# A perceiver layer on one core: batch 0's scores moved ahead in the self attention, values as the stationary operand, residual sums before their norms, filling matmuls placed anew

## The chip, the cores and the metric

The kernel runs on one core of a Trainium2 chip. The metric is device time in microseconds. Three runs of the kernel before took 890.71, 892.66 and 893.37 us, median 892.66 us. Most executions of one kernel agree within 0.3 per cent (2.7 us here).

The engines of the core are TensorE (PE in the rows; its weight loads are PEld), VectorE (DVE), ScalarE (ACT), GpSimd (POOL) and SyncE (SP), which here issues nearly all DMAs. Each runs its own list of instructions in order, and they wait for each other by semaphores.

## The reference, cut to what matters

Everything is float32. B = 2 batches, L = 128 latent rows, D = 512 columns.

```
x = x + xattn(ctx_1024, layernorm(x), mask, ...)      # latents attend to 2048 context rows, 16 heads of 64
x = x + attn(layernorm(x), qw, kw, vw, ow)            # the self attention, where the change lies
x = x + ffn(layernorm(x), ...)                        # gated MLP of 2048, and product-key experts

def attn(x, qw, kw, vw, ow):                          # 16 heads of 32, batch 2, sequence 128
    Q, K, V = rope(x @ qw), rope(x @ kw), x @ vw
    score = Q @ K^T / sqrt(32) - 1e10 * (1 - causal)  # 128 x 128 for each head
    weights = softmax(score)
    return (weights @ V) @ ow
```

## The kernel before, in words

The program is written out by hand for each engine. Nothing is scheduled by a planner: the order of the calls in each engine's block is the order in which the engine works, and semaphores (`s_...`, `c_...` for compute, `d_...` for DMAs) tie the blocks together. Activations and weights of most products are kept as a high and a low part, and `product` (L1619 to L1623) issues three matmuls: high by high, high by low, low by high. An operand is split by a copy on ScalarE (`..._hi`) and a subtraction on VectorE (`..._lo`, L1096).

The span has three parts. The cross attention (from 0 to about 654 us) runs 48 iterations of a pair of heads. The self attention (about 652 to 716 us) is what the change rewrites. The feed-forward part (gated MLP, then 16 steps of experts) fills the rest. The weight blocks of the last two parts come by DMA (2 MB each where they are split already) into a few slots of SBUF, each issued once the block that used the slot last has been used (`wait_used`).

At the very start TensorE turns the first context chunk and the latents (`x_turn`, `latent`), and between these calls it runs ten matmuls whose results nobody reads: `occupy`, L1782 to L1785, filling matmuls that keep the engine busy. Then come the first query product `queries(0)` and the first keys `project_keys(0, 0)`.

The self attention works like this, b being the batch:

- `turn_rows` transposes a normalised 128x512 activation on TensorE in four pieces into a PSUM bank from `TBANK`. ScalarE's `transposed_hi` and VectorE's `transposed_lo` split it into `HT` (the input), `QTs` (queries), `KN` (keys) or `AT` (the attention's output).
- `project_rows(m, b)` is a product over four blocks of 128, twelve matmuls of 128x512: m = 0 queries, 1 keys, 2 values. `rotate(m, b)` applies the rotary embedding on VectorE; `values_hi(b)` copies the values to `VV` on ScalarE.
- `scores(b)` makes all 16 heads' scores in 48 matmuls of 32 rows. `row_max(g)` (VectorE, g = 4b + c, four heads each) adds the mask and takes the maximum, `exps(g)` (ScalarE) makes four exponentials with their sums, `turn_weights(g)` (TensorE) transposes them, `probs_copy(g)` copies them to `PV2`, and `weigh_values(g)` multiplies by the values.
- In the kernel before, `weigh_values` takes the 128x128 weights of a head as the stationary operand and streams 32 columns of values: the output has latent rows on partitions. VectorE's `norm_outputs(b)` divides by the sums (`AO`), and `turn_rows(AO, b)` transposes again before `mix_rows(b)`, the product with `ow`.
- `add_rows(i, b)` adds to the residual and takes the row statistics, GpSimd's `row_rstd(i, b)` makes the inverse deviation, `norm_rows(i, b)` normalises.

Around the stage's end VectorE's order is `norm_outputs(1)`, `add_rows(1, 0)`, `transposed_lo(AT, 1)`, `norm_rows(1, 0)`, the two low parts of the search keys `KBk`, `transposed_lo(HT, 0)`, `add_rows(1, 1)`, `norm_rows(1, 1)`, `transposed_lo(HT, 1)`. TensorE then makes the search queries (product with `fWq`, L1621 on `pS<-XA,WS`), with which the feed-forward part begins.

Of the kernel before, what the change touches and what calls it, by code (L numbers as in the profile page):

```python
# [26 lines left out]
ALU = mybir.AluOpType  # L27
ACT = mybir.ActivationFunctionType
AX = mybir.AxisListType

P = 128
# [4 lines left out]
def perceiver_layer(nc, x, ctx1024, mask, g1, b1, g2, b2, Wq, Wkv, Wout, qw, kw, vw, ow,  # L36
# [40 lines left out]
    with ExitStack() as stack:  # L77
# [155 lines left out]
        s_ao = sem("s_ao")  # L233
# [62 lines left out]
        AO = QR  # L296
# [33 lines left out]
        TBANK = (pJ[:, 0, :], pJ[:, 0, :], pT[:, 1, :], pX, pX, pV, pX, pV, pX, pV)  # L330
# [64 lines left out]
        def _(sp):  # L395
# [180 lines left out]
            sp.wait_ge(s_tt, 10)  # L576
# [26 lines left out]
        def _(pool):  # L603
# [133 lines left out]
            gp.memset(KV[:, 0:1024].bitcast(U32), 0).then_inc(s_kz, 1)  # L737
            pool.wait_ge(s_sc, 8)
# [8 lines left out]
            last.then_inc(s_iota, 1)  # L747
            for b in range(B):
                row_rstd(1, b)
# [17 lines left out]
        def _(act):  # L767
# [198 lines left out]
            def transposed_hi(dst, b):  # L966

                act.wait_ge(s_tt, nb[0] + 1)
                ac.activation(dst[:, HI, :, L * b:L * b + L], TBANK[nb[0]].rearrange("p (c t) -> p c t", c=4), ACT.Copy).then_inc(s_th, 1)
                nb[0] += 1  # L970

            def values_hi(b):
# [4 lines left out]
                ac.activation(VV[:, b, :], (pT[:, 0, :], pJ[:, 0, :])[b], ACT.Copy).then_inc(s_vh, 1)  # L977
# [8 lines left out]

            joined_hi(ITERS - 2)
            transposed_hi(HT, 0)
            joined_hi(ITERS - 1)
            transposed_hi(HT, 1)  # L990
            transposed_hi(QTs, 0)
            values_hi(0)
            transposed_hi(KN, 0)
            exps(0)
            exps(1)
            values_hi(1)
            transposed_hi(QTs, 1)
            transposed_hi(KN, 1)
            for g in range(2, 8):
                exps(g)  # L1000
            transposed_hi(AT, 0)
            transposed_hi(AT, 1)
# [82 lines left out]
        def _(dve):  # L1085
# [274 lines left out]
            def rotate(m, b):  # L1360
# [5 lines left out]
                z = ((pS[:, 0, :], pS[:, 1, :]), (pV, pJ[:, 1, :]))[b][m].rearrange("p (h e two) -> p h e two", h=SH, two=2)  # L1366
# [26 lines left out]
            def probs_copy(g):  # L1393
# [4 lines left out]
                ve.tensor_copy(PV2[:, g % 4, :], pJ[:, (g + 1) % 2, :]).then_inc(s_p2h, 1)  # L1398
# [38 lines left out]
            probs_copy(5)
            transposed_lo(AT, 0)
            probs_copy(6)
            probs_copy(7)  # L1440
            norm_outputs(1)
            add_rows(1, 0)
            transposed_lo(AT, 1)
            norm_rows(1, 0)
            dve.wait_ge(s_kh, 1)
# [3 lines left out]
            transposed_lo(HT, 0)  # L1449
            add_rows(1, 1)  # L1450
            norm_rows(1, 1)
            transposed_lo(HT, 1)
# [163 lines left out]
        def _(pe):  # L1616
# [165 lines left out]
            def occupy(bank, weights, moving, n):  # L1782

                for _ in range(n):
# [378 lines left out]
```

## Time and profile before

| what | value |
|---|---|
| median of three runs | 892.66 us |
| the profiled execution | 892.87 us, span 891.1 us, so 1.8 us lie outside the span |
| TensorE busy | 851.9 us (96%) |
| VectorE, ScalarE, GpSimd busy | 579.7 us (65%), 437.5 us (49%), 349.0 us (39%) |
| granted TensorE clock, mean | 0.995 of full speed |
| the chain of waits, by engine | PE 81%, DVE 10%, issue 3%, ACT 3%, DMA 2%, POOL 1% |

The span counts from the first instruction to the last. A matmul's end is modelled and matmuls are pipelined, so a full TensorE is not one at its peak. Filling matmuls count as busy. Line numbers are those of the kernel before.

### The profile page before, as it was taken

Reading aid. Unit: us, or ns where it says so; the run is one execution under the profiler, and the core shown is the slowest. Engines: PE = TensorE matmul, PEld = TensorE weight load, DVE = VectorE, ACT = ScalarE, POOL = GpSimd, SP = SyncE. Lnnn points to the kernel's source line nnn. Section 1 sums busy time; section 2 is a strip of 40 time slices with the busy share of each in tenths; the row PEclk is TensorE's granted clock in tenths of the full one; section 3 lists DMA queues with packets and bytes.
Section 4 is the critical chain, followed back from the end, with each engine's and each line's share of the span. In section 5 each row is a group of like instructions: output and inputs, shape, how many; then the busy total and the mean of one; then the engine's idle time right before and its main releaser. Section 6 shows DMA issues by size and latency. Waiting matters only on the chain.

```text
span 891.1 us, 17432 instructions
## 1 busy us (share of the span) xinstructions
PE 851.9 (96%) x6353; PEld 794.7 (89%) x6353; DVE 579.7 (65%) x1540; ACT 437.5 (49%) x1017; POOL 349.0 (39%) x362
## 2 busy tenths in 40 slices
PE   3899999999999999999999999999989999998997
PEld 2889999999999999999999999999967789987885
DVE  7445555566576878756566666777767546746885
ACT  4465554545546455544646454455425224334552
POOL 5634523645353664745454453413211110003442
PEclk9999999999999999999999999999999999999999
DMA  6365336457566677575666755887578366842310
GB/s 200 95 221 172 120 130 224 177 192 231 197 237 239 242 234 272 200 236 195 234 215 213 238 192 191 292 336 246 207 295 329 136 257 262 352 143 89 101 48 25
DMA packets 71109, 183.04 MB, mean 205 GB/s; under 512 B 6336, under 2 KB 19568, under 8 KB 65008
## 3 DMA queue, kind: packets, MB, share of 16 engines
q1 hardware_dynamic: 70928, 181.90, 57.8%
q8 instruction: 51, 0.84, 0.4%
q14 instruction: 34, 0.28, 0.1%
q10 hardware_dynamic: 96, 0.02, 0.0%
HBM read 130.00 MB, written 50.86 MB: 203 GB/s over the span
## 4 chain that ended last, share of the span: by engine, by line
PE 81%; DVE 10%; issue 3%; ACT 3%; DMA 2%; POOL 1%; SPq 0%; DVEq 0%; ACTq 0%; POOLq 0%
PE pJ L1621 15%; PE pJ L1622 14%; PE pJ L1623 14%; PE pV L1751 8%; PE pS L1729 4%; PE pT L1737 3%; PE pS L1737 3%; PE pT L1729 2%; PE pS L1621 2%; PE pS L1622 2%; PE pS L1623 2%; PE pX L1652 1%; DVE late L1578 1%; DMA WS<-w_split 1%; PE pV L1621 1%
## 5 line engine op out<-in xcount | busy, mean ns | idle before, releaser
L1621 PE MATMUL pJ<-WV,XT 128*128 128x256 f32 x544 | 159.2, 293 | 0.0
L1622 PE MATMUL pJ<-WV,XT 128*128 128x256 f32 x544 | 154.5, 284 | 0.0
L1623 PE MATMUL pJ<-WV,XT 128*128 128x256 f32 x544 | 154.4, 284 | 0.0
L848 ACT ACTIVATE SP<-SP,xneg 128x768 f32<-128x768 f32 (+1 forms) x96 | 85.8, 895 | 119.5 <-DVE xneg L1200 119.5
L1621 PE MATMUL pJ<-XT,WK 128*128 128x384 f32 (+1 forms) x384 | 126.9, 330 | 3.9 <-DVE VT L1096 2.9
L1623 PE MATMUL pJ<-XT,WK 128*128 128x384 f32 (+1 forms) x384 | 125.2, 326 | 0.0
L1622 PE MATMUL pJ<-XT,WK 128*128 128x384 f32 (+1 forms) x384 | 125.1, 326 | 0.0
L1096 DVE TENSOR_TENSOR KT<-pJ,KT 128x384 fp32r<-128x384 f32 x96 | 51.1, 535 | 90.8 <-ACT KT L825 90.3
L1621 PEld LDWEIGHTS pJ<-WV,XT 128*128 128x128 f32 x544 | 104.8, 193 | 0.5 <-issue 0.2
L1622 PEld LDWEIGHTS pJ<-WV,XT 128*128 128x128 f32 x544 | 104.9, 193 | 0.0
L1623 PEld LDWEIGHTS pJ<-WV,XT 128*128 128x128 f32 x544 | 104.8, 193 | 0.0
L649 POOL TENSOR_TENSOR XT<-xtmp,XT 128x384 fp32r<-128x384 f32 (+1 forms) x44 | 41.4, 940 | 135.8 <-ACT XT L809 135.6
L832 ACT ACTIVATE VT<-pJ 128x512 fp32r<-128x512 f32 (+1 forms) x72 | 41.2, 573 | 86.8 <-PE pJ L1623 86.8
L825 ACT ACTIVATE KT<-pJ 128x384 fp32r<-128x384 f32 x96 | 44.9, 469 | 69.1 <-PE pJ L1623 69.1
L1751 PE MATMUL pV<-PT,VT 128*128 128x256 f32 x544 | 77.5, 291 | 0.0
L1621 PEld LDWEIGHTS pJ<-XT,WK 128*128 128x128 f32 x384 | 72.3, 188 | 5.6 <-DVE VT L1096 4.4
L1751 PEld LDWEIGHTS pV<-PT,VT 128*128 128x128 f32 x544 | 67.6, 189 | 10.2 <-issue 8.0
L1096 DVE TENSOR_TENSOR VT<-pJ,VT 128x512 fp32r<-128x512 f32 (+1 forms) x72 | 47.2, 656 | 40.0 <-ACT VT L832 39.6
L1622 PEld LDWEIGHTS pJ<-XT,WK 128*128 128x128 f32 x384 | 72.4, 189 | 0.0
L1623 PEld LDWEIGHTS pJ<-XT,WK 128*128 128x128 f32 x384 | 72.2, 188 | 0.0
L1194 DVE CUSTOM_DVE_ANT_0 SP<-pS,MB,mx 128x384 f32<-128x384 f32 x64 | 36.9, 615 | 50.8 <-PE pS L1729 50.8
L759 POOL TENSOR_TENSOR late<-late 128x512 f32<-128x512 f32 x16 | 20.6, 1288 | 111.9 <-DVE late L1578 111.9
(374 smaller groups left out, 2171.5 us busy)
## 6 DMA issues: line engine op xcount, KB each, us to landing
WS<-w_split SPq DMA_DIRECT2D x14, 2048.0 KB, 8.9
WV<-wv_split SPq DMA_DIRECT2D x20, 1024.0 KB, 7.0
WK<-wk_split SPq DMA_DIRECT2D x40, 512.0 KB, 4.4
w_split<-wkst SPq DMA_DIRECT2D x40, 512.0 KB, 3.3
w_split<-wvst SPq DMA_DIRECT2D x40, 512.0 KB, 3.8
XA<-w_split SPq DMA_DIRECT2D x4, 2048.0 KB, 12.9
xraw<-in_ctx SPq DMA_DIRECT2D x7, 768.0 KB, 6.4
wk_split<-WK SPq DMA_DIRECT2D x8, 512.0 KB, 3.8
```

The lines of the kernel that those rows point to most:

```text
L649: gp.tensor_tensor(XT[:, C % 4, LO, k, c0:c0 + w], xtmp[:, e % 2, 0:w], XT[:, C % 4, HI, k, c0:c0 + w].bitcast(F32), ALU.subtract).then_in ...
L825: ac.activation(KT[:, q, HI, 0:w], pJ[:, j % 2, 0:w], ACT.Copy).then_inc(c_jh, 1)
L832: ac.activation(VT[:, G % 2, ts[0]:ts[-1] + 1, :, HI, :], pJ[:, j % 2, 0:256 * len(ts)].rearrange("p (t h e) -> p t h e", t=len(ts), h=4), ...
L848: ac.activation(SP[:, I % 2, h, 0:w], SP[:, I % 2, h, 0:w], ACT.Exp, bias=xneg[:, I % 2, h:h + 1], scale=XSC, accum_out=total).then_inc(c_ ...
L1096: return ve.tensor_tensor(dst, src, hi.bitcast(F32), ALU.subtract)
L1194: ve.tensor_tensor_reduce(out=SP[:, n % 2, h, c0:c0 + w], in0=BANK[2 * q + h][:, 0:w], in1=MB[:, c0:c0 + w], scale=1.0, scalar=before, op0 ...
L1621: te.matmul(dst, a(HI), b(HI), start=start, stop=False)
L1622: te.matmul(dst, a(HI), b(LO), start=False, stop=False)
L1623: return te.matmul(dst, a(LO), b(HI), start=False, stop=stop)
L1729: last = te.matmul(BANK[2 * q + h][:, 0:w], Q[rows, qs, p, :], KT[rows, q, ks, 0:w], start=o == 0, stop=o == 2)
L1737: last = te.transpose(BANK[t % 4][:, P * i:P * i + P], SP[:, I % 2, h, CWID * q + P * i:CWID * q + P * i + P], ident[:, :])
L1751: last = te.matmul(pO[:, h, :, :], VT[:, G % 2, 3 * q + i, 2 * (I % 2) + h, :, :], PTS[t % 4][:, :, P * i:P * i + P], start=q == 0 and i = ...
```

## The change

It has five parts, all by hand.

1. The ten filling matmuls ahead of `queries(0)` are gone.
2. In the self attention the queries and keys of batch 0 are rotated, turned and split before the input of batch 1 is, and `scores(0)` comes before any product of batch 1. The value product of batch 0 and that of batch 1 are cut into halves with turns between them. The four `probs_copy` of batch 0 move from VectorE to ScalarE. `transposed_lo(KN, 1)` now stands ahead of `row_max(4)` to `row_max(7)`, which follow each other without copies between.
3. `weigh_values` takes 32 columns of values as the stationary operand and streams the 128 columns of turned weights; head h of the four writes partitions 32h to 32h + 31. The output comes out transposed, so `turn_rows(AO, b)` is dropped. For the division the inverse sums must be on the other axis: VectorE's `invert`, GpSimd's `repeat_inverses` (a copy that repeats each inverse 32 times), TensorE's `turn_inverses` (four transposes), ScalarE's `inverse_rows` (a copy to SBUF), then VectorE multiplies in place in PSUM and ScalarE's `weighed_hi` and the low part follow.
4. `add_rows(1, 1)` stands ahead of `norm_rows(1, 0)`, and the low parts of `KBk` behind both splits of `HT`.
5. The filling matmuls of the self attention are 4 + 3 + 3 + 3 inside and 9 + 2 + 5 before the search queries (before: 4 + 4 + 4 + 4 + 4, and 16 + 5); the five behind the search queries stay.

```diff
-        AO = QR
+        IROW = QR
+        RBANK = (pV[:, :], pS[:, 0, :])
...
-        TBANK = (pJ[:, 0, :], pJ[:, 0, :], pT[:, 1, :], pX, pX, pV, pX, pV, pX, pV)
+        TBANK = (pJ[:, 0, :], pT[:, 1, :], pX, pJ[:, 0, :], pJ[:, 1, :], pV, pX, pV, pX, pV)
+        PBANK = (pJ[:, 0, :],) * 4 + (pJ[:, 1, :], pJ[:, 0, :]) * 2
...
+            def repeat_inverses(b):
+
+                pool.wait_ge(s_inv, b + 1)
+                gp.tensor_copy(an[:, b, :].rearrange("p (h e) -> p h e", h=SH),
+                               small[:, 32 + 16 * b:48 + 16 * b].unsqueeze(2).broadcast_to([P, SH, SD])).then_inc(s_rep, 1)
...
+            def probs_copy(g):
+
+                act.wait_ge(s_pt2, g + 1)
+                ac.activation(PV2[:, g % 4, :], PBANK[g], ACT.Copy).then_inc(s_p2h, 1)
+
+            def inverse_rows(b):
+
+                act.wait_ge(s_row, b + 2)
+                ac.activation(IROW[:, b, :], RBANK[b], ACT.Copy).then_inc(s_rowc, 1)
...
             def norm_outputs(b):
 
-                dve.wait_ge(s_se, 4 * b + 4)
-                inv = small[:, 32 + 16 * b:48 + 16 * b]
-                link(ve.reciprocal(inv, small[:, 16 * b:16 * b + 16]))
+                dve.wait_ge(s_rowc, b + 2)
                 dve.wait_ge(s_pv2, 4 * b + 4)
-                ve.tensor_tensor(AO[:, b, :].rearrange("p (h e) -> p h e", h=SH), OUT2[b].rearrange("p (h e) -> p h e", h=SH),
-                                 inv.unsqueeze(2).broadcast_to([P, SH, SD]), ALU.mult).then_inc(s_ao, 1)
+                ve.tensor_tensor(OUT2[b][:, :], OUT2[b][:, :], IROW[:, b, :], ALU.mult).then_inc(s_ao, 1)
...
             def weigh_values(g):
 
                 b, c = g // 4, g % 4
+                pe.wait_ge(s_vh, b + 1)
                 pe.wait_ge(s_p2h, g + 1)
                 for h in range(4):
                     cs = slice(SD * (4 * c + h), SD * (4 * c + h) + SD)
-                    last = te.matmul(OUT2[b][:, cs], PV2[:, g % 4, P * h:P * h + P], VV[:, b, cs], start=True, stop=True)
+                    last = te.matmul(OUT2[b][ROWS4[h], P * c:P * c + P], VV[:, b, cs], PV2[:, g % 4, P * h:P * h + P], start=True, stop=True)
                 last.then_inc(s_pv2, 1)
...
+            def turn_inverses(b):
+
+                pe.wait_ge(s_rep, 4 + b + 1)
+                if b == 1:
+                    pe.wait_ge(s_sm, 8)
+                for c in range(4):
+                    last = te.transpose(RBANK[b][:, P * c:P * c + P], an[:, b, P * c:P * c + P], ident[:, :])
+                last.then_inc(s_row, 1)
```

TensorE around the first scores, before: the last products of a whole projection of batch 1's keys (`pJ<-WS,XA`), then the scores (`pS` and `pT<-KNs,XA`, 24 such rows), then the values of batch 1.

```order
L1621 MATMUL pJ<-WS,XA 128x512
L1622 MATMUL pJ<-WS,XA 128x512
L1623 MATMUL pJ<-WS,XA 128x512
L1903 MATMUL pS<-KNs,XA 128x128 x2
L1903 MATMUL pT<-KNs,XA 128x128 x2
```

The same place in the changed kernel (L1906 are transposes of `late`, the rotated keys, and `raw`, the input of batch 1):

```order
L1906 MATMUL pX<-ident,late 128x128 x4
L1906 MATMUL pJ<-ident,raw 128x128 x4
L1656 MATMUL pV<-WS,XA 128x512
L1657 MATMUL pV<-WS,XA 128x512
L1658 MATMUL pV<-WS,XA 128x512
L1656 MATMUL pV<-WS,XA 128x512
L1657 MATMUL pV<-WS,XA 128x512
L1658 MATMUL pV<-WS,XA 128x512
L1935 MATMUL pS<-KNs,XA 128x128 x2
L1935 MATMUL pT<-KNs,XA 128x128 x2
```

Only the second half of batch 0's values is left ahead of the scores, and batch 1's queries and keys have moved behind them.

TensorE from the second batch's first weighed values to the product with `ow` (`pX<-WS,XA`), before:

```order
L1927 MATMUL pX<-xst,PVs 128x32 x8
L1785 MATMUL pJ<-WS 128x512 x4
L1918 MATMUL pJ<-ident,SMs 128x128 x4
L1876 MATMUL pX<-ident,late 128x128 x4
L1918 MATMUL pJ<-ident,SMs 128x128 x4
L1927 MATMUL pV<-xst,PVs 128x32 x8
L1785 MATMUL pJ<-WS 128x512 x4
L1918 MATMUL pJ<-ident,SMs 128x128 x8
L1927 MATMUL pV<-xst,PVs 128x32 x8
L1621 MATMUL pX<-WS,XA 128x512
```

and in the changed kernel (L1948 turns weights, L1958 weighs values, L1967 turns inverses, L1900 fills):

```order
L1948 MATMUL pJ<-ident,SMs 128x128 x4
L1958 MATMUL pV<-PVs,xst 32x128 x4
L1900 MATMUL pJ<-WS 128x512 x3
L1948 MATMUL pJ<-ident,SMs 128x128 x4
L1958 MATMUL pV<-PVs,xst 32x128 x4
L1900 MATMUL pJ<-WS 128x512 x3
L1948 MATMUL pJ<-ident,SMs 128x128 x4
L1967 MATMUL pS<-ident,O 128x128 x4
L1958 MATMUL pV<-PVs,xst 32x128 x8
L1656 MATMUL pX<-WS,XA 128x512
```

The turns go singly and the last turn is followed by the inverses; the turn of the output (L1876) is gone.

VectorE at the end of the stage, before (`XA<-pV` and `XA<-pX` are low parts, `O<-xres` the norms):

```order
L1406 TENSOR_TENSOR late<-pV,small 128x512
L1257 TENSOR_TENSOR xres<-pX,xres 128x512
L1258 BN_STATS st<-xres 128x6
L1259 BN_AGGR mv<-st 128x2
L1096 TENSOR_TENSOR XA<-pV,XA 128x4x128
L1264 TENSOR_SCALAR O<-xres,mv,rstd 128x512
L1096 TENSOR_TENSOR KV<-pT,KV 64x4x64 x2
L1096 TENSOR_TENSOR XA<-pX,XA 128x4x128
L1257 TENSOR_TENSOR xres<-pV,xres 128x512
L1258 BN_STATS st<-xres 128x6
L1259 BN_AGGR mv<-st 128x2
L1264 TENSOR_SCALAR O<-xres,mv,rstd 128x512
```

and in the changed kernel:

```order
L1444 TENSOR_TENSOR pV<-pV,late 128x512
L1131 TENSOR_TENSOR XA<-pV,XA 128x4x128
L1292 TENSOR_TENSOR xres<-pX,xres 128x512
L1293 BN_STATS st<-xres 128x6
L1294 BN_AGGR mv<-st 128x2
L1292 TENSOR_TENSOR xres<-pV,xres 128x512
L1293 BN_STATS st<-xres 128x6
L1294 BN_AGGR mv<-st 128x2
L1299 TENSOR_SCALAR O<-xres,mv,rstd 128x512 x2
L1131 TENSOR_TENSOR XA<-pX,XA 128x4x128
L1131 TENSOR_TENSOR XA<-pV,XA 128x4x128
L1131 TENSOR_TENSOR KV<-pT,KV 64x4x64 x2
```

The low part of the second output is now first, and the second residual sum has nothing but the first in front of it.

## Rows read from the trace of the kernel before

**Rows 1.** The page, part 4: the chain by engine

```profile
PE 81%; DVE 10%; issue 3%; ACT 3%; DMA 2%; POOL 1%; SPq 0%; DVEq 0%; ACTq 0%; POOLq 0%
```

**Rows 2.** Windows: length, busy PE, PEld, DVE, ACT, POOL, clock, DMA, GB/s

```profile
20.10:22.00 1.90, 1.69 (x12) 1.49 (x12) 1.83 (x5) 1.40 (x4) 1.82 (x3) 1.00 1.03 387
28.00:33.00 5.00, 5.00 (x33) 5.00 (x32) 2.50 (x7) 2.60 (x5) 2.02 (x2) 0.66 0.19 56
660.00:716.20 56.20, 49.65 (x359) 40.55 (x357) 36.44 (x131) 19.19 (x77) 8.33 (x20) 1.00 0.67 269
```

**Rows 3.** Timeline, TensorE at the start: start, length, instruction, idle before and releaser

```profile
12.06 2.06 PE L1785 MATMUL pS<-WQs 128*128 128x512 f32 x4
...
20.15 0.38 PE L1621 MATMUL pJ<-XL,WQs 128*128 128x256 f32 x1 [1.35 <-POOL XL L673]
...
22.92 0.41 PE L1621 MATMUL pJ<-XT,WK 128*128 128x384 f32 x1 [1.08 <-issue]
...
27.49 0.55 PE L1652 MATMUL pX<-ident,Oacc 128*128 128x128 f32 x3 [2.24 <-ACT Oacc L913]
```

**Rows 4.** Timeline, VectorE in the self attention

```profile
662.01 0.39 DVE L1370 TENSOR_TENSOR late<-pS,rope 128x256 f32<-128x256 f32 x1
...
664.22 0.55 DVE L1264 TENSOR_SCALAR raw<-xres,mv,rstd 128x512 f32<-128x512 f32 x1
...
686.25 0.29 DVE L1386 CUSTOM_DVE_ANT_0 SMs<-pS,cmask 128x128 f32<-128x128 f32 x1 [1.30 <-PE pT L1903]
...
687.30 0.28 DVE L1386 CUSTOM_DVE_ANT_0 SMs<-pS,cmask 128x128 f32<-128x128 f32 x1
...
710.89 0.68 DVE L1257 TENSOR_TENSOR xres<-pV,xres 128x512 f32<-128x512 f32 x1
...
713.58 0.55 DVE L1264 TENSOR_SCALAR O<-xres,mv,rstd 128x512 f32<-128x512 f32 x1 [1.06 <-POOL rstd L730]
```

**Rows 5.** Timeline, TensorE in the self attention, and one row of the experts

```profile
663.75 0.50 PE L1621 MATMUL pT<-WS,XA 128*128 128x512 f32 x1 [0.69 <-DMA WS<-w_split]
...
674.84 0.32 PE L1903 MATMUL pS<-KNs,XA 32*128 32x128 f32 x2
...
684.56 0.33 PE L1903 MATMUL pS<-KNs,XA 32*128 32x128 f32 x2
...
686.05 1.97 PE L1927 MATMUL pX<-xst,PVs 128*128 128x32 f32 x16
687.86 1.19 PE L1785 MATMUL pJ<-WS 128*128 128x512 f32 x4
...
700.82 0.48 PE L1621 MATMUL pX<-WS,XA 128*128 128x512 f32 x1
...
706.12 0.50 PE L1621 MATMUL pV<-WS,XA 128*128 128x512 f32 x1 [1.47 <-DVE XA L1096]
...
709.02 0.60 PE L1876 MATMUL pX<-ident,O 128*128 128x128 f32 x4
709.37 3.90 PE L1785 MATMUL pS<-WS 128*128 128x512 f32 x16
...
716.25 0.39 PE L1621 MATMUL pS<-XA,WS 128*128 128x256 f32 x1 [0.27 <-DVE XA L1096]
...
806.61 0.69 PE L2116 MATMUL pS<-exrow,delta 1*128 1x256 f32 x2
```

**Rows 6.** Timeline, ScalarE: the last pair of exponentials and what follows it

```profile
691.93 0.40 ACT L983 ACTIVATE SMs<-SMs,negm 128x128 f32<-128x128 f32 x1 [1.31 <-DVE negm L1391]
...
695.03 0.58 ACT L969 ACTIVATE XA<-pX 128x512 fp32r<-128x512 f32 x1
```

**Rows 7.** Groups by form, GpSimd: count, busy us, mean ns, idle before

```profile
L661 POOL TENSOR_SCALAR xraw<-xraw,mv,rstd 128x512 f32<-128x512 f32 x27 | 56.2, 2095 | 0.9
...
L625 POOL CAST wvst<-wvst 128x512 fp32r<-128x512 f32 x40 | 25.3, 633 | 2.3 <-DMA wvst<-in_L_ffn_Wu 1.6 <-DMA wvst<-in_L_ffn_Wg 0.4 <-DMA wvst<-in_L_attn_qw 0.2
```

**Rows 8.** The page, part 6: weight blocks, KB each, us to landing

```profile
WS<-w_split SPq DMA_DIRECT2D x14, 2048.0 KB, 8.9
```

More of the change, by code:

```diff
@@ L989, in _ @@
             joined_hi(ITERS - 1)
+            transposed_hi(QTs, 0)
+            transposed_hi(KN, 0)
             transposed_hi(HT, 1)
-            transposed_hi(QTs, 0)
             values_hi(0)
-            transposed_hi(KN, 0)
             exps(0)
             exps(1)
+            probs_copy(0)
+            exps(2)
+            probs_copy(1)
+            transposed_hi(QTs, 1)
+            exps(3)
+            transposed_hi(KN, 1)
+            probs_copy(2)
             values_hi(1)
-            transposed_hi(QTs, 1)
-            transposed_hi(KN, 1)
-            for g in range(2, 8):
+            probs_copy(3)
+            exps(4)
+            inverse_rows(0)
+            for g in range(5, 8):
                 exps(g)
-            transposed_hi(AT, 0)
-            transposed_hi(AT, 1)
+            weighed_hi(0)
+            inverse_rows(1)
+            weighed_hi(1)
             act.wait_ge(s_kt, 1)
@@ L1780, in latent @@
                 last.then_inc(c_lt, 1)
-            def occupy(bank, weights, moving, n):
-                for _ in range(n):
-                    te.matmul(bank, weights, moving, start=True, stop=True)
-            first_q = WQs[:, 0, HI, :, :].rearrange("p k n -> p (k n)")
             x_turn(0, 0)
             x_turn(0, 1)
-            pe.wait_ge(c_wqh, 1)
-            occupy(pS[:, 0, :], WQs[:, 0, HI, 0, :], first_q, 4)
             latent(0)
             latent(1)
-            occupy(pS[:, 0, :], WQs[:, 0, HI, 0, :], first_q, 2)
             latent(2)
@@ L1870, in _, with occupy @@
                     queries(I + 2)
+            def occupy(bank, weights, moving, n):
+                for _ in range(n):
+                    te.matmul(bank, weights, moving, start=True, stop=True)
             def turn_rows(src, b, ready, count):
@@ L1877, in turn_rows @@
                 last.then_inc(s_tt, 1)
-                nb[0] += 1
+                nb[0] += 3 if nb[0] == 5 else 1
             def last_rows(k0, k1, joined):
@@ L1950, in _ @@
+            project_rows(0, 1)
+            turn_weights(0)
+            pe.wait_ge(s_vh, 1)
             project_rows(1, 1)
-            scores(0)
-            project_rows(2, 1)
             turn_rows(QR, 1, s_rope, 3)
+            turn_weights(1)
+            weigh_values(0)
+            pe.wait_ge(s_sm, 4)
+            project_rows(2, 1, (0, 1))
             turn_rows(KR, 1, s_rope, 4)
-            turn_weights(0)
-            weight_ready(5)
-            pe.wait_ge(s_vh, 2)
-            occupy(pJ[:, 0, :], slot4(5, HI)[:, 0, 0:P], slot4(5, HI)[:, 0, :], 4)
@@ L1959, in _ @@
-            turn_weights(1)
-            pe.wait_ge(s_tl, 5)
-            occupy(pX[:, :], slot4(5, HI)[:, 0, 0:P], slot4(5, HI)[:, 0, :], 4)
-            scores(1)
-            weigh_values(0)
+            turn_weights(2)
             weigh_values(1)
-            occupy(pJ[:, 1, :], slot4(5, HI)[:, 0, 0:P], slot4(5, HI)[:, 0, :], 4)
-            turn_weights(2)
+            project_rows(2, 1, (2, 3))
             turn_weights(3)
             weigh_values(2)
+            scores(1)
+            turn_inverses(0)
```

132 lines of the change are left out of this document (74 added, 58 removed).

## The prediction, made before the changed kernel ran

> **What bounds the kernel now.** I read the chain of waits by engine first: TensorE holds 81% of it [rows 1]. So what counts is where TensorE waits, and the windows show it: in the stretch from 660.0 to 716.2 us, the self attention, it is busy 49.65 of 56.2 us, the granted clock is 1.00, and DMA is at 0.67 [rows 2]. That busy time flatters the stretch, since it counts filling matmuls, 16 of which take 3.90 us, 0.24 us each, in front of the search queries [rows 5]. The timeline shows three waits. The first scores start at 674.84 us; the second at 684.56; VectorE can begin the second softmax only at 686.25, after 1.30 us idle [rows 4, 5]. ScalarE's exponentials of batch 1 are interrupted (1.31 us idle before the last pair) and end at 695.03 [rows 6]. The product with `ow` of batch 0 starts at 700.82, that of batch 1 only at 706.12 after waiting 1.47 us for a low part, and the search queries at 716.25 [rows 5]. All four are ends of one serial story, so I walk it again in the new order. Outside it nothing of the order of work changes except at the start.
>
> **Unit prices.** A product of twelve matmuls behind a wait: 709.02 - 706.12 = 2.90 us, and 2.85 without one; half of it 1.45. Four transposes: 709.37 - 709.02 = 0.35, I take 0.40 with the change of operands. 48 score matmuls: 686.05 - 684.56 = 1.49. Two `weigh_values` in the old form: 687.86 - 686.05 = 1.81, 0.90 each [rows 5]. A `row_max`: 687.30 - 686.25 = 1.05. A rotation: 664.22 - 662.01 = 2.2. A residual sum with statistics: 713.58 - 710.89, less the 1.06 of waiting for GpSimd, 1.6. A norm: 0.55 [rows 4]. An `exps`: (695.03 - 691.93) / 2 = 1.55; a ScalarE copy: 0.58, 0.48 when others follow [rows 6]. I add 0.1 to 0.2 us for each semaphore between engines.
>
> **Batch 0's scores first.** TensorE ends the keys of batch 0 at 663.1 (663.75 less 0.69 of waiting) as before. Rotation (0,0) now stands ahead of the residual sum, so queries are ready at 660.9 and turned at 663.5; the value weights land at 663.7, where TensorE waited for them before [rows 5], and half the value product runs to 665.2. VectorE: residual sum to 662.5, rotation (1,0) 663.1 to 665.3, norm of batch 1's input to 665.9. Keys turned at 665.8, split at 667.4; in between TensorE turns batch 1's input and does the other value half, to 667.75. Scores start at 667.75, 7.1 us sooner than 674.84.
>
> **Up to the second scores.** From 669.25 TensorE has three projections of batch 1 (3 x 2.85), five turns (2.0), three `weigh_values` and two or three short waits. With 0.6 us for a weighing that is 8.55 + 2.0 + 1.8 + 0.8 = 13.2, so the second scores start at 682.5 instead of 684.56: 2.0 us. ScalarE (four `exps`, three copies of 0.48, three splits and the values: 9.9 us from 670.6) and VectorE are done just before. The moved 7.1 us are mostly spent here: the same TensorE work, but now under batch 0's softmax instead of ahead of it.
>
> **Batch 1's softmax.** VectorE has the four `row_max` in a row, 684.2 to 688.4, and ScalarE then never waits: `exps(4)` from 685.4, four times 1.55 plus one copy of the turned inverses 0.48, end 692.1 against 695.03. That is 2.0 from before, 1.3 for the idle that is gone, 0.48 given back: 2.9 us in all. Cover: turns, weighings and fills lie under the exponentials.
>
> **Up to the product with `ow`.** Before, from 695.03 to 700.82, 5.8 us: two turns of weights after a late weighing and fills, two copies, two weighings of 0.9. Now only `turn_weights(7)` and the inverses are left: turn 693.1, inverse sums ready at 692.5, GpSimd's copy, turned inverses, two weighings of 0.6: product at 695.1. So 3.0 us from 692.1 to 695.1, a gain of another 2.8; 5.7 in all. GpSimd's copy is not in the trace: its plain copy of 128x512 takes 0.63 and its two-scalar operation on the same size 2.10 [rows 7]. I take 0.65, as it has one input; then TensorE's turns of `exps(7)` cover nearly all of it. The upper end costs 1.4 us.
>
> **From one `ow` product to the other.** 5.3 us before: product 2.85, turn, ScalarE's split, and the low part behind a residual sum on VectorE. The second output now needs no turn and its low part stands first, so it is split (697.3) before the first product ends (697.95); then the keys' turn 0.4 and the product at 698.4 instead of 706.12. 2.0 us more, 7.7 in all.
>
> **To the search queries.** Product ends 701.25. From the residual sum at 710.89 to the queries at 716.25 took 5.36 us, and this chain (sum, GpSimd, norm, turn, split, low part) stays as it is, with batch 0's norm lying in GpSimd's share. But before, the sum began 1.9 us behind the product's end (709.02), because a low part stood ahead of it; now 0.15. Queries at 701.3 + 5.4 = 706.7 us, against 716.25: 9.5 us. The low parts of `KBk` (0.85 us) lie under the queries.
>
> **The weighing.** The new form is in no row. Its bounds: 48 score matmuls of 128 columns on a quarter of the array come every 31 ns (1.49 / 48), which with eight passes and an entry of about 0.25 gives 0.5 us; the one fp32 product with a wide moving operand takes 0.69 us for its two passes of 256 columns [rows 5], without the entry 0.11 us for 128 columns and a pass, so eight passes one after the other and the entry give 1.1; the old 0.90 lies between. I take 0.6, near the score row because here too each quarter of the array has its own operand. Five weighings lie on the path: -0.5 to +2.5 us. On TensorE's side the trace shows only row groups running together. The Trainium skill (TensorEngine Tiling (Array Packing), Tiling Modes, Key Properties) says that tiles work in parallel but that "Changing tiling mode (not just tile) drains the TensorE"; the first half speaks for the low bound, the second against the change, since every weighing now goes into such a mode and out. No row here prices a switch with 32 columns of output.
>
> **The start.** The first four fillers took 2.06 us, 0.51 each against 0.24 later, so TensorE was at its lower level of 1.2 GHz then; the first query product ran at the full clock; the values of 28 to 33 us, after idling 2.24 us, have a granted clock of 0.66 [rows 2, 3, 5]. Without fillers queries (twelve of 256 columns) and keys (twelve of 384) would run at half rate: they begin at 20.2 and 23.0, the keys end by 27.0 and the turns wait for ScalarE until 27.49 anyway [rows 3]. So the loss is hidden, by at least 0.4 us. And TensorE, then busy to 27 rather than 25, may keep or get the full clock for the values: 5 us at 0.66 hold 1.7 us to win; if it stays low longer, 1.0 to lose. I take 0.5 gained. The Trainium skill (TensorE: Matmul & The Clock Gate, Part 4) holds that transposes don't count as work for the clock; by that the queries do start at half rate, and the sum is the same by it.
>
> **Hidden ends.** The feed-forward's weights: a block lands 8.9 us after its issue [rows 8]; the first gate block's issue goes by batch 1's keys (1 us later than before), more than 25 us ahead of its use, and later ones go by uses that move along.
>
> **Sum.** 892.87 (the profiled execution; the median, 892.66, is 0.2 under it) - 9.5 - 0.5 = 882.9 us.
>
> **Rivals.** (a) *Weighing and inverses dear.* Weighings of 1.1 and a GpSimd copy of 2.1 us: 882.9 + 2.5 + 1.4, about 886.8. For it: no row for either. Against: one-input copies of this size are all 0.63. 13%. (b) *The gain is not passed on*: the stage ends sooner but the first gate products or experts wait for weights or selections, leaving under 2.7 us: about 891. Against: in the rows of the self attention's end only compute releases TensorE. 4%. (c) *Slower, by the clock.* Six gaps of 0.5 to 1 us on TensorE between 685 and 695 with fewer fillers (29 against 41) lower the granted clock to 1.2 GHz from there to the search queries. The path then holds about 2 x 2.9 of `ow`, 3 of weighings and turns and 5.8 of search queries at double time: 14 us lost, 897. It decides from the point where the low clock covers 9.5 us or more of TensorE work on the path. Against: the stretch kept 1.00 with a busy share of 0.88 [rows 2], and the gaps I find are no longer than its own. 4%. (d) *More gained*: weighings at 0.5 and all values at full clock, 881.2; 12%. (e) The walk holds: 67%.
>
> **Chances and range.** This kernel's runs tell 0.3% (2.7 us) from no change. Faster: e, a, d and nothing else, 0.92; same: b, 0.04; slower: c, 0.04. Range: d's low edge 880.5 to a's end 887.0.
>
> **What would show it.** Right: first scores near 667.8, second near 682.5, ScalarE's last exponential ending near 692, `ow` products at 695 and 698.4, search queries at 706.7 of the span. A weighing's four matmuls (eight passes) read in one row of the timeline; GpSimd's `small` copy likewise. Wrong if TensorE's idle before `turn_inverses(1)` exceeds 0.3 us, if the windows from 685 to 707 show a clock under 1.00, or if the distance from the search queries to the end, 174.8 us before, grows.

## The result, and the profile after

The changed kernel takes 881.38 us (median of 4 runs, 880.55 to 882.77), the kernel before, run beside it, 893.01. The ratio is 0.9866 with an interval of 0.9826 to 0.9906: 11.6 us by the medians or 1.3% faster, where 10.0 and a time of 882.9 had been forecast. On another chip, in a later comparison (`after_again` below), the ratio was 0.9882 (0.9865 to 0.9900), 10.5 us. One of the twelve executions of `start_fill_off` below took 4682.81 us and isn't counted in its ratio.

The profiled execution took 880.55 us, the shortest of the four; its span is 878.8 us. First the page's chain by engine, which answers to [rows 1]:

```profile
PE 79%; DVE 8%; DMA 4%; issue 3%; ACT 3%; POOL 1%; SPq 1%; DVEq 0%; ACTq 0%; POOLq 0%
```

TensorE still sets the end. The windows that answer to [rows 2] (length, busy PE, PEld, DVE, ACT, POOL, clock, DMA share, GB/s):

```profile
20.10:22.00 1.90, 1.82 (x8) 1.82 (x9) 1.86 (x5) 1.45 (x3) 1.82 (x4) 1.00 0.77 278
28.00:33.00 5.00, 5.00 (x42) 4.58 (x41) 2.81 (x10) 4.16 (x8) 3.24 (x4) 1.00 0.02 5
660.00:703.40 43.40, 40.46 (x334) 29.64 (x332) 29.67 (x117) 22.58 (x83) 9.39 (x21) 1.00 0.77 306
```

The second line is new: the values at the start run at a clock of 1.00 where it was 0.66. The clock of the first can't be taken at its word: the products in it come every 0.21 to 0.22 us, as the rows below show (20.56, 20.78), where the same product of 256 columns comes every 0.12 us at the full clock (31.22, 31.34 us), so they run at the lower level. The third line is busy for 0.93 of its time, against 0.88.

TensorE in the self attention, by the timeline (start, length, instruction, idle before and releaser); the rows answer to [rows 5]:

```profile
652.25 0.50 PE L1656 MATMUL pS<-WS,XA 128*128 128x512 f32 x1 [0.86 <-DVE XA L1131]
...
664.99 0.33 PE L1935 MATMUL pS<-KNs,XA 32*128 32x128 f32 x2
...
673.24 0.60 PE L1948 MATMUL pJ<-ident,SMs 128*128 128x128 f32 x4
673.77 0.42 PE L1958 MATMUL pX<-PVs,xst 128*32 128x128 f32 x8
674.13 0.50 PE L1656 MATMUL pT<-WS,XA 128*128 128x512 f32 x1
...
679.35 0.33 PE L1935 MATMUL pS<-KNs,XA 32*128 32x128 f32 x2
...
683.92 0.66 PE L1948 MATMUL pJ<-ident,SMs 128*128 128x128 f32 x4 [0.94 <-ACT SMs L993]
...
686.03 0.63 PE L1948 MATMUL pJ<-ident,SMs 128*128 128x128 f32 x4 [0.76 <-DVE PVs L1433]
...
690.56 0.77 PE L1958 MATMUL pV<-PVs,xst 128*32 128x128 f32 x16
691.41 0.50 PE L1656 MATMUL pX<-WS,XA 128*128 128x512 f32 x1
...
694.79 0.50 PE L1656 MATMUL pV<-WS,XA 128*128 128x512 f32 x1
...
703.42 0.38 PE L1656 MATMUL pS<-XA,WS 128*128 128x256 f32 x1 [0.26 <-DVE XA L1131]
```

VectorE and ScalarE there, by the same view, answering to [rows 4] and [rows 6]:

```profile
681.04 0.29 DVE L1421 CUSTOM_DVE_ANT_0 SMs<-pS,cmask 128x128 f32<-128x128 f32 x1 [3.19 <-PE pT L1935]
...
697.85 0.69 DVE L1292 TENSOR_TENSOR xres<-pV,xres 128x512 f32<-128x512 f32 x1 [1.70 <-PE pV L1658]
```

```profile
688.87 0.58 ACT L1010 ACTIVATE XA<-pX 128x512 fp32r<-128x512 f32 x1
```

VectorE waits for the second scores longer than before (3.19 us against 1.30 [rows 4]), and batch 1's residual sum follows its product with nothing between. TensorE's first row is a product ahead of all that moved in this stage. The same product started at 655.12 us before:

```profile
655.12 0.49 PE L1621 MATMUL pS<-WS,XA 128*128 128x512 f32 x1 [0.86 <-DVE XA L1096]
```

So 2.87 us had been gained by then, at the start; to compare the stage with my walk, they are added back:

| step | before | predicted | after | after + 2.87 |
|---|---|---|---|---|
| first scores | 674.84 | 667.75 | 664.99 | 667.86 |
| second scores | 684.56 | 682.5 | 679.35 | 682.22 |
| ScalarE's last exponential ends | 695.03 | 692.1 | 688.87 | 691.74 |
| product with `ow`, batch 0 | 700.82 | 695.1 | 691.41 | 694.28 |
| product with `ow`, batch 1 | 706.12 | 698.4 | 694.79 | 697.66 |
| search queries | 716.25 | 706.7 | 703.42 | 706.29 |

The stage gave 9.96 us where 9.5 stood in the sum, the start 2.87 where 0.5 stood, and the rest took 175.4 us instead of 174.8, within its scatter (174.1 to 176.2 over fourteen profiles). Together 12.3 us of span. Two prices that no row had shown are read above and here: a weighing is 0.36 us (673.77 to 674.13; 690.56 to 691.41 holds two and a wait), and GpSimd's copy is 0.61, both times that it runs:

```profile
677.92 0.61 POOL L743 COPY O<-small 128x512 f32<-128x512 f32 x1 [16.61 <-DVE small L1438]
```

The start is where my working missed. TensorE after:

```profile
14.72 0.69 PE L1814 MATMUL pX<-ident,SP 128*128 128x128 f32 x2 [2.32 <-DVE SP L1175]
...
20.18 0.58 PE L1656 MATMUL pJ<-XL,WQs 128*128 128x256 f32 x1 [1.63 <-POOL XL L675]
20.56 0.42 PE L1657 MATMUL pJ<-XL,WQs 128*128 128x256 f32 x1
20.78 0.42 PE L1658 MATMUL pJ<-XL,WQs 128*128 128x256 f32 x1
...
25.95 0.55 PE L1687 MATMUL pX<-ident,Oacc 128*128 128x128 f32 x3
```

The queries run at half rate, as forecast. But the turns of `Oacc` come at 25.95 us, straight behind the keys, and not at 27.49 [rows 3]. What they wait for is ScalarE's norm, and that waits for VectorE's `nmr`. ScalarE in the kernel before:

```profile
25.21 2.22 ACT L913 ACTIVATE Oacc<-Oacc,nmr,rstd 128x512 f32<-128x512 f32 x3 [2.89 <-DVE nmr L1296]
```

VectorE in the kernel before:

```profile
17.15 1.03 DVE L1123 CAST XT<-OF 128x256 fp32r<-128x256 f32 x2
...
20.99 1.84 DVE L1096 TENSOR_TENSOR XT<-Oacc,XT 128x256 fp32r<-128x256 f32 x2
22.75 2.30 DVE L1096 TENSOR_TENSOR WV<-wvst,WV 128x1024 fp32r<-128x1024 f32 x1
24.97 0.15 DVE L1296 SCALAR_TENSOR_TENSOR nmr<-mv,rstd 128x3 f32<-128x3 f32 x1
```

and after:

```profile
17.13 0.50 DVE L1158 CAST XT<-OF 128x256 fp32r<-128x256 f32 x2
...
20.52 0.76 DVE L1131 TENSOR_TENSOR XT<-Oacc,XT 128x256 fp32r<-128x256 f32 x2
21.20 1.22 DVE L1131 TENSOR_TENSOR WV<-wvst,WV 128x1024 fp32r<-128x1024 f32 x1
22.33 1.24 DVE L1331 SCALAR_TENSOR_TENSOR nmr<-mv,rstd 128x3 f32<-128x3 f32 x1
```

The same low part takes 2.30 or 1.22 us, the small `nmr` 0.15 or 1.24. GpSimd in the kernel before and after shows what lies beside them:

```profile
21.24 1.30 POOL L637 TENSOR_TENSOR WQs<-wqst,WQs 128x512 fp32r<-128x512 f32 x1
22.50 1.47 POOL L633 TENSOR_TENSOR WK<-wkst,WK 128x512 fp32r<-128x512 f32 x1
```

```profile
21.66 1.89 POOL L639 TENSOR_TENSOR WQs<-wqst,WQs 128x512 fp32r<-128x512 f32 x1
```

As the rows read, the two engines hold each other up, and the row that starts second is the long one. Before, GpSimd's `WK` row starts first (22.50) and VectorE's low part is long. After, VectorE's part starts first (21.20), GpSimd's row is long (1.89), and `nmr`, begun at 22.33, is done only when that row ends, 23.55 us. `before_nmr_first` below shows the same pair the other way round. That it is access to memory which one engine withholds from the other is not shown by any run here. The Trainium skill (Advanced Engine Details and Errata, VectorE Performance Modes) says of VectorE's two-port instructions that they and GpSimd's "will interfere/block eachother", since the second port is shared; its table there gives `tensor_tensor` no two-port mode, so for the subtraction here, 2.30 against 1.22 us, it is near the case and doesn't state it.

What shifted their meeting is small: ScalarE's first split of the latents starts at 15.45 us instead of 15.23, because the transposes ahead of it run at the low clock now, and GpSimd's rows behind it shift by the same 0.22. The two VectorE sequences part at the cast of `XT` in the rows above: before it lies beside a GpSimd row that starts at 17.24 and takes 1.03 us for its two, after it is over in 0.50 before GpSimd's starts at 17.46. By the turns of `Oacc` it is worth 1.5 us.

### The profile page after: what moved, and what is told of

It is laid out like the page before. It is cut to its first block, busy times and chain, and to the rows that moved or that the text cites. A ratio compares the mean times of both kernels' runs of the same rounds, so it can differ in the third digit from the quotient of the medians.

```text
span 878.8 us, 17399 instructions
## 1 busy us (share of the span) xinstructions
PE 844.0 (96%) x6331; PEld 785.3 (89%) x6331; DVE 575.0 (65%) x1536; ACT 440.7 (50%) x1023; POOL 350.7 (40%) x364
## 4 chain that ended last, share of the span: by engine, by line
PE 79%; DVE 8%; DMA 4%; issue 3%; ACT 3%; POOL 1%; SPq 1%; DVEq 0%; ACTq 0%; POOLq 0%
PE pJ L1656 14%; PE pJ L1657 14%; PE pJ L1658 14%; PE pV L1786 7%; PE pS L1764 4%; PE pT L1772 3%; PE pS L1772 3%; PE pT L1764 2%; PE pS L1656 2%; PE pS L1658 2%; PE pS L1657 2%; DMA w_split<-wvst 1%; PE pX L1687 1%; DVE late L1613 1%; PE pV L1656 1%
```

## The experiments

Twelve runs in three comparisons, each with its own runs of the kernel before on the same chip; ratios are to these. "Stage" is the distance from the first scores to the search queries in the profile: 38.43 us in the changed kernel.

### The start: start_fill_back, start_fill_off, before_nmr_first, fill_nmr_first

```diff
             x_turn(0, 1)
+            pe.wait_ge(c_wqh, 1)
+            occupy(pS[:, 0, :], WQs[:, 0, HI, 0, :], first_q, 4)
             latent(0)
             latent(1)
+            occupy(pS[:, 0, :], WQs[:, 0, HI, 0, :], first_q, 2)
...
             x_turn(0, 3)
+            occupy(pS[:, 0, :], WQs[:, 0, HI, 0, :], first_q, 4)
             queries(0)
```

> The changed kernel with the ten filling matmuls put back ahead of the first query product; all else as changed. Theory A (the fillers cost the whole 2.9 us seen in the first 33 us): about 881.4 + 2.9 = 884.3 us, first scores of the cross attention at 33.3 us of the span, a granted clock near 0.66 in the values and VectorE's nmr near 25.0. Theory B (the part of it that comes from VectorE, 1.5 us, is a matter of how its operations fall beside GpSimd's in one execution and not of the fillers): about 882.9, the scores at 31.8.

Ratio 0.9882 (0.9862 to 0.9903), 883.7 us, but from 880.21 to 885.63 over five runs. The profiled one is the 880.21, and it speaks against theory A's mechanism: with the fillers in place the turns start at 25.99 us and `nmr` is early. The median lies near theory A's 884.3, but the five spread too far to tell it from 882.9. Its clock came late: a pair of latent transposes takes 0.69 us, as without fillers (0.44 before).

```profile
14.76 0.69 PE L1814 MATMUL pX<-ident,SP 128*128 128x128 f32 x2 [0.62 <-DVE SP L1175]
...
25.99 0.55 PE L1687 MATMUL pX<-ident,Oacc 128*128 128x128 f32 x3 [1.99 <-ACT Oacc L923]
```

So the fillers don't cost the 2.9 us each time. As I read it, they make it a matter of the execution whether the clock has risen by 14.7 us; where it has, the transposes are fast and VectorE meets GpSimd badly. The second half rests on one profile: of the four with these fillers only that of the kernel before has the fast transposes.

The reverse, the ten fillers taken out of the kernel before:

> The kernel before without its ten filling matmuls ahead of the first query product, nothing else changed. Theory A: 893.0 - 2.9 = 890.1 us, ScalarE's Oacc norm from 23.7 instead of 25.2 us and all values at the full clock. My forecast's term said 0.5 us (892.5). Rival: the self attention's new order carries all of the gain and the start nothing, 893.0.

0.9970 (0.9954 to 0.9986): 2.7 us faster, 1.3 to 4.1. Theory A's 2.9 lies in the interval, my forecast's 0.5 does not. The profile has the turns at 26.01 us and the cross attention's first scores at 30.34, as the changed kernel has (30.28), against 33.31 before.

```diff
-            dve.wait_ge(c_wvh, 1)
-            low(WV[:, 0, LO], wvst[:, :, :], WV[:, 0, HI]).then_inc(c_wv0, 1)
             dve.wait_ge(c_rstd, 2)
             ve.scalar_tensor_tensor(nmr[:, 0:3], ...).then_inc(s_nmr, 1)
+            dve.wait_ge(c_wvh, 1)
+            low(WV[:, 0, LO], wvst[:, :, :], WV[:, 0, HI]).then_inc(c_wv0, 1)
```

> The kernel before, fillers kept, with VectorE's nmr (what ScalarE's norm of Oacc waits for) ahead of WV's low part instead of behind it. If it is VectorE's late nmr that held the turns to 27.49 us, the turns start when the keys end (25.3), TensorE no longer idles 2.24 us, and with the full clock in the values (1.7 us) up to 3.9 us come back: 889.1 us. If only the clock counted and it stays at 0.66, 2.2 us: 890.8. If the turns wait for something else: 893.0.

0.9978 (0.9965 to 0.9991): 2.0 us faster, 0.8 to 3.1. In the profile the turns start at 25.25 us and the cross attention's first scores at 29.58, so its start is 3.7 us better than the one profiled before. But the clock came late in this execution too (0.69 us for a pair of latent transposes), so the profile doesn't show the collision avoided: the turns are 0.7 us sooner than `start_fill_back`'s. The case for `nmr` is the median of twelve: with the fillers kept, its place alone brought 2.0 us. The median got less than 3.7, probably because not every execution of the kernel before meets the collision. And here VectorE's low part starts just ahead of GpSimd's `WK` row, keeps its length, and GpSimd's is the long one, against 2.30 and 1.47 in the kernel before:

```profile
22.80 1.21 DVE L1096 TENSOR_TENSOR WV<-wvst,WV 128x1024 fp32r<-128x1024 f32 x1
```

```profile
22.81 2.33 POOL L633 TENSOR_TENSOR WK<-wkst,WK 128x512 fp32r<-128x512 f32 x1
```

> The changed kernel with the ten fillers back and nmr ahead of WV's low part: queries and keys at the full clock (keys end 25.3 instead of 25.9) and the turns not held. Expected 0.6 us faster than the changed kernel, 880.8, if both theories of the start hold; 884.3 if nmr's place is without effect; 882 to 883 if the low clock in the values comes back all the same.

0.9853 (0.9834 to 0.9871), 880.92 us, 880.16 to 882.62: the lowest median of all runs, and 880.8 was expected. Its interval overlaps with both of the changed kernel's, so that it is better isn't shown.

### The weighing: after_again, old_weigh_form

> The changed kernel itself, as the measure for the three others on the same chip. Expected: 0.987 of the kernel before, and in most executions full clock and early nmr at the start, since without fillers the transposes ahead of the queries are slow each time.

0.9882 (0.9865 to 0.9900), 882.65 us. The start was as expected (turns at 26.12), but the profile brought what my rival (c) had described: the clock fell inside batch 1's softmax, behind the same two gaps of 0.94 and 0.76 us that the other execution had passed at 1.00.

```profile
682.00:686.90 4.90, 3.54 (x31) 2.12 (x23) 4.51 (x37) 3.47 (x16) 4.16 (x12) 1.00 0.99 415
687.00:690.30 3.30, 3.06 (x16) 1.98 (x17) 1.47 (x3) 3.30 (x19) 0.81 (x2) 0.54 1.01 425
```

The second line has 0.54, about the lower level of 1.2 GHz; from 690.4 to 706.0 us it is 0.99 again. Stage: 39.92 instead of 38.43, so 1.49 us of this kernel's time come and go with it. A clock under 1.00 between 685 and 707 us was one of my signs of being wrong; this execution shows it, the other doesn't.

```diff
-   te.matmul(OUT2[b][ROWS4[h], P * c:P * c + P], VV[:, b, cs], PV2[:, g % 4, P * h:P * h + P], ...)
+   te.matmul(OUT2[b][:, cs], PV2[:, g % 4, P * h:P * h + P], VV[:, b, cs], ...)
```

> The changed kernel with weights as stationary operand again in the eight weighings (the old form: 32 columns moving through 128 by 128), so the weighed values come out untransposed and what is copied from them is another number; everything else is as changed. Theory A: the form's price, 0.90 us in place of 0.36, lies on the path for the three weighings ahead of the second scores and the last two, 5 x 0.54 = 2.7 us slower than the changed kernel. Theory B: the weighings wait for the copies of the turned weights anyway, so at most the last two count: 1.1 us or less.

0.9898 (0.9883 to 0.9913), 884.16 us, 1.5 us over `after_again` by the medians. The profiles say it more sharply, since the start and the clock drop out: the stage is 40.78 us against 38.43. The second scores are 1.12 us later, the first product with `ow` 2.39. This is theory A, a little under its 2.7: one weighing is 0.91 us in the old form, but enters 0.09 us sooner behind a turn (0.44 instead of 0.53).

```profile
681.52 0.60 PE L1948 MATMUL pJ<-ident,SMs 128*128 128x128 f32 x4
681.96 0.98 PE L1958 MATMUL pX<-xst,PVs 128*128 128x32 f32 x8
682.87 0.33 PE L1935 MATMUL pS<-KNs,XA 32*128 32x128 f32 x2
```

### The tail: tail_old, tail_both

```diff
-            transposed_lo(AT, 1)
             add_rows(1, 0)
-            add_rows(1, 1)
+            transposed_lo(AT, 1)
             norm_rows(1, 0)
-            norm_rows(1, 1)
-            transposed_lo(HT, 0)
-            transposed_lo(HT, 1)
...
+            transposed_lo(HT, 0)
+            add_rows(1, 1)
+            norm_rows(1, 1)
+            transposed_lo(HT, 1)
```

(the dots are `KBk`'s low parts)

> The changed kernel with VectorE's last steps in the old order: batch 0's residual sum ahead of the second output's low part, KBk's low parts and batch 0's norm and low part ahead of batch 1's sum. Theory A (my sum: 2.0 us at the second product with ow and 1.7 at the residual sum): the second product starts 1.9 to 2.0 us later, the search queries 3.5 to 3.7 us later. Theory B: the waits of the tail are hidden by TensorE's fillers and GpSimd's share, under 1 us.

0.9957 (0.9943 to 0.9971), 6.3 us over `after_again`. The second product is 1.99 us later, as in theory A, but the stage is 44.90 us, 6.5 longer. Neither theory fits: TensorE was left in the new order, where nine fillers stand ahead of batch 0's turn, and VectorE's low part of that turn now stands ahead of batch 1's residual sum. So the sum waited for fillers, and behind the idle time the clock fell to 0.50 between 706.8 and 710.1 us.

```profile
703.20 0.69 DVE L1131 TENSOR_TENSOR XA<-pX,XA 128x512 fp32r<-128x512 f32 x1 [4.07 <-ACT XA L979]
703.80 0.68 DVE L1292 TENSOR_TENSOR xres<-pV,xres 128x512 f32<-128x512 f32 x1
```

Hence the same with TensorE's order undone too:

```diff
-            occupy(pT[:, 1, :], searcher[:, 0:P], searcher, 9)
             turn_rows(hn, 0, s_src, 3)
-            occupy(pT[:, 1, :], searcher[:, 0:P], searcher, 2)
+            occupy(pT[:, 1, :], searcher[:, 0:P], searcher, 11)
```

> VectorE's last steps in the old order as in tail_old, and TensorE's too (batch 0's turn straight behind the second product with ow, all fillers behind it). Theory A: the extra 3 us of tail_old came from this mismatch, and the old tail on both engines costs what I had summed: second product 1.9 to 2.0 us later, search queries 41.9 us behind the first scores instead of 38.4, so 3.5 us slower than the changed kernel. Theory B: the old tail costs 6 us also with TensorE's order, and my sum was short by half.

0.9918 (0.9889 to 0.9946), 887.3 us: 5.4 us over `nmr_more_fill` on the same chip, 3 to 5 us over the changed kernel by the ratios. The second product is 1.94 us later. The stage is 43.43 instead of the expected 41.9, and the windows have the difference: the new wait of 1.91 us was followed by a fall of the clock in the middle of the product.

```profile
698.98 0.50 PE L1656 MATMUL pV<-WS,XA 128*128 128x512 f32 x1 [1.91 <-DVE XA L1131]
```

```profile
686.00:699.80 13.80, 10.88 (x81) 7.51 (x82) 8.46 (x27) 7.65 (x32) 4.06 (x9) 1.00 0.70 292
699.90:703.20 3.30, 3.30 (x10) 2.51 (x9) 1.17 (x3) 0.00 (x0) 0.00 (x0) 0.50 0.03 7
```

3.3 us at 0.50 and busy throughout hold 1.65 us; 43.43 - 1.65 = 41.8. Theory A's price of the old tail holds, with the clock's share on top. Its other half, that 3 us of `tail_old` were the mismatch, doesn't come out of the profiles: the two stages are 1.5 us apart (44.90 and 43.43, each with one fall of the clock), the ratios 3.5 us with intervals that just touch.

### The early scores: late_scores, late_scores_both

```diff
-            scores(0)
             pe.wait_ge(s_tl, 4)
             project_rows(0, 1)
-            turn_weights(0)
             pe.wait_ge(s_vh, 1)
             project_rows(1, 1)
+            scores(0)
+            turn_weights(0)
             turn_rows(QR, 1, s_rope, 3)
```

> The changed kernel with batch 0's scores behind the query and key products of batch 1 instead of ahead of them (5.7 us later, same instructions). Theory A (the early scores let the softmax of batch 0 run under batch 1's products): second scores 2.0 to 2.5 us later because three exponentials, copies and weighings of batch 0 then end last, and all later times with them. Theory B (TensorE has the same work either way, the order is worth nothing): no change within 0.3 us.

0.9961 (0.9944 to 0.9978), 7.6 us over `after_again`: both theories are wrong. The scores start at 672.64 us (`after_again` 666.20), and from them to the second scores it still takes 15.76 us (14.36), because TensorE waits twice:

```profile
677.21 0.80 PE L1948 MATMUL pJ<-ident,SMs 128*128 128x128 f32 x4 [3.01 <-ACT SMs L993]
679.72 1.11 PE L1906 MATMUL pJ<-ident,late 128*128 128x128 f32 x4 [1.71 <-DVE late L1410]
```

The first wait is for batch 0's exponentials, with nothing left to lay under them; the second for a rotation that stands behind three `row_max` on VectorE. And from 677.2 to 684 us the clock is at 0.53.

```diff
+            rotate(0, 1)
             row_max(0)
             row_max(1)
             row_max(2)
-            rotate(0, 1)
             row_max(3)
             rotate(1, 1)
```

(on top of `late_scores`)

> Batch 0's scores behind two products of batch 1 as in late_scores, and VectorE's rotation of batch 1's queries ahead of the four row_max instead of behind three, so that TensorE's turn of them no longer waits 1.7 us. Theory A: late_scores lost 1.4 us of its 8 to that wait and to the clock, so this one is 5 to 6 us slower than the changed kernel (first scores 6.9 us later, 12.5 to 13.5 instead of 14.4 us from there to the second). Theory B (the order of the scores is worth only what I had counted up to the second scores): 2.0 us slower.

0.9928 (0.9901 to 0.9955), 887.98 us: 6.1 us over `nmr_more_fill`, 4 to 6 over the changed kernel by the ratios. The wait for the rotation is gone, that for the exponentials stays at 3.12 us, and from the first to the second scores it takes 13.43 us, as theory A has it. Behind the wait the clock falls once more:

```profile
676.70:680.00 3.30, 3.21 (x16) 2.48 (x20) 3.20 (x18) 3.30 (x16) 0.00 (x0) 0.50 1.03 439
```

Counted from the turn of batch 0's queries, which both kernels start alike (661.21 and 662.54 us), the second scores are 4.8 us later than in `nmr_more_fill` (24.29 against 19.50). The wait is 3.12 of that and the clock 1.6: the products of batch 1 lie under batch 0's softmax or they don't.

### The fillers: nmr_more_fill, no_fill_att

The first has the start's edit of `before_nmr_first` and

```diff
-            occupy(PBANK[4], mixer[:, 0:P], mixer, 4)
+            occupy(PBANK[4], mixer[:, 0:P], mixer, 7)
...
-            occupy(PBANK[5], mixer[:, 0:P], mixer, 3)
+            occupy(PBANK[5], mixer[:, 0:P], mixer, 5)
```

> The changed kernel with two repairs: VectorE's nmr ahead of WV's low part at the start, and five more filling matmuls in batch 1's softmax (7 in place of 4 ahead of turn_weights(4), 5 in place of 3 ahead of turn_weights(5)), which cover 1.2 of the 1.7 us that TensorE idles there. If those gaps are what lets the clock fall in some executions (1.5 us lost in the self attention of after_again), no execution here shows a low stretch between 680 and 700 us and the median is 1 to 1.5 us under the changed kernel's, about 0.986 of the kernel before; if the fall comes elsewhere anyway, no difference from 0.988.

0.9862 (0.9835 to 0.9889), 881.86 us. The gaps shrank from 0.94 and 0.76 us to 0.24 and 0.30 (at 686.60 and 688.71 us), no low stretch lies in the self attention (stage 38.40), and the runs lie close (881.52 to 882.69, mean clock 0.997 or 0.998 in all six; `after_again` had 880.13 to 884.32 and 0.995 to 1.000). But the median isn't shown to be lower: in this profile the clock fell at 46 us, in the cross attention, instead. The 1.2 us more of fillers cost nothing.

```profile
46.10:49.40 3.30, 3.30 (x13) 3.21 (x12) 0.77 (x4) 2.56 (x6) 0.29 (x1) 0.53 1.04 362
660.00:706.00 46.00, 44.03 (x350) 32.74 (x348) 31.60 (x122) 22.55 (x83) 9.77 (x22) 1.00 0.77 310
```

The second leaves out all 29 fillers from batch 1's softmax to the search queries:

> The changed kernel without any of the 29 filling matmuls of the self attention's second half. Theory A (my rival c: fillers keep the clock): the granted clock falls to its lower level in the stretch from about 684 us to the search queries in every execution, and the path there loses 3 to 8 us: 885 to 890. Theory B (the fillers are padding; the products keep the clock): within 0.5 us of the changed kernel.

0.9885 (0.9857 to 0.9913), 884.07 us, 2.2 us over `nmr_more_fill`. The clock does fall, in two stretches of the profile, and the mean clock of all six runs is 0.989 to 0.993:

```profile
687.90:694.60 6.70, 6.08 (x48) 3.87 (x48) 3.99 (x7) 4.62 (x21) 1.81 (x4) 0.52 0.99 416
694.70:704.90 10.20, 7.28 (x41) 5.16 (x33) 5.54 (x11) 1.96 (x4) 1.78 (x4) 0.99 0.40 138
705.00:711.70 6.70, 5.29 (x25) 4.90 (x25) 2.01 (x4) 0.60 (x1) 0.00 (x0) 0.52 1.00 426
```

This is theory A in its mechanism, under its lower end in size: the first stretch lies mostly beside ScalarE's exponentials, so the first product with `ow` is only 1.0 us later, and the second lies on the search queries.

## Why the prediction was right, point by point

- *The number.* The mechanism carries it, and some compensation and luck of the draw lie on top. In the profiled pair the start gave 2.4 us more than its term, the stage 0.5 more, and what follows took 0.5 back, so 12.3 us came where 10.0 stood. The profiled execution was the shortest of its four, with no fall of the clock in the stage; `after_again`, with one, is at 10.5 us.
- *The serial story of the self attention.* Right within 0.8 us at each of the six places of the table. `late_scores_both` and `tail_both` put about 5 us (1.6 of it the clock) and 3.4 us (without the clock) on its two orders, `old_weigh_form` 2.4 on the weighing. They aren't added up, since each was undone alone.
- *The weighing.* 0.36 us where I took 0.6 and bounded from 0.5 to 1.1: the mis-sized term, below its low end. I had built the bound from passes of 31 ns plus an entry of 0.25; the rows give 0.36 for the eight passes with all. The page cited for a drain at a change of tiling mode (the Trainium skill, TensorEngine Tiling (Array Packing), Key Properties) speaks against this form; the trace shows 0.09 us on the way in, by which it enters later behind a turn, and whatever the way out costs lies within the 0.36. With two weighings ahead of the first `ow` product, this is 0.5 of the 0.8 us that it came sooner than my walk.
- *GpSimd's copy.* 0.61 measured, 0.65 taken; TensorE has no idle time before `turn_inverses(1)`. Covered, as said. Rival (a) falls on both prices.
- *The tail.* 1.99 and 1.94 us at the second product against my 2.0, and 3.4 at the search queries (43.43 - 1.65 against 38.43) against 3.5 to 3.7.
- *The start.* The step that failed is "the turns wait for ScalarE until 27.49 anyway". I took 27.49 as fixed; it hung on the order in which VectorE and GpSimd met. The gain was 2.87 us in the profiled pair and 2.7 (1.3 to 4.1) by `start_fill_off`, against the 0.5 taken and the 1.7 that I had as its best. Of the 2.9, 1.5 are `nmr` and the rest is the clock in the values, the part I had named (from the turns to the cross attention's first scores 4.33 us against 5.82). The late clock cost the queries what I had said and the keys less (they end at 25.9 and not 27.0), and it stayed hidden: in `start_fill_back` the keys are done 2 us sooner and the turns start at 25.99 all the same.
- *Rival (c), the clock.* I had it at 4% and it isn't refuted: it occurs in one of the two profiles of the changed kernel, but for some 3 us of time and 1.5 us of loss and not for the 14 us that I priced. Its condition was half right (two gaps of that length, 0.94 and 0.76 us, where I had named six), its size was not.
- *What follows the stage.* 174.1 to 176.2 us in all profiles: nothing was given back there, so rival (b) falls.

## What to carry to other kernels

When one batch's softmax and another's projections share the engines, issue the scores as soon as their operands exist and put the projections behind them: worth about 5 us here, of which 3.1 are the wait that reappears and 1.6 the fall of the clock behind it. Undo or move such an order on all engines at once, because the engine left behind adds a wait of its own (`tail_old`: a stage of 44.9 us, `tail_both`: 43.4, each with one fall of the clock). And a start time that an engine "waits for anyway" is only fixed if each operation ahead of it is: compare the length of the same instruction elsewhere before counting on it.

## What the runs showed of the hardware that was not expected

- VectorE's and GpSimd's elementwise operations hold each other up, and in the profiles read here the row that starts first keeps its length or nearly (GpSimd's 1.47 in the kernel before), while the other ends about its own length behind it: VectorE's 128x1024 takes 2.30 us when it starts 0.25 behind GpSimd's row, 1.22 and 1.21 when it starts first; GpSimd's 128x512 then takes 1.89 and 2.33 instead of 1.28 to 1.30; a 128x3 operation on VectorE takes 1.24 against 0.15. A slip of 0.2 us ahead of them moved the turns of `Oacc` by 1.5.
- The granted clock of the changed kernel fell from 687.0 to 690.3 us in one profile, behind idle times of 0.94 and 0.76 us, and not in the other, behind the same idle times. In the kernel before it fell from 28.4 to 31.7 us, behind 2.24 us, and in `nmr_more_fill` from 46.1 to 49.4 us. In `start_fill_back` the same fillers brought the full clock later than in the kernel before. So a profile shows one draw. The spread of 4 to 8 us in the runs of the kernel before is probably in part such draws: on one chip its shortest run, 891.47 us, has a mean clock of 0.998 and its longest, 899.54, one of 0.991. What decides in a single execution stays open.
- One thing more stays open: from the cross attention's first scores to those of the self attention the profiles of the new order differ by 2.5 us (634.3 to 636.8 us, `nmr_more_fill` with its fall of the clock left out), without a cause that I can name.
